# Layout transfers behind a block's first loads, gaps between scatters and expert blocks, routing spread over a block's groups, zero experts added by ScalarE

## The chip, the cores and the metric

The program runs on 1 core of one Trainium2 chip. The metric is device time in microseconds (us), median of the runs. ScalarE is called ACT here, VectorE DVE, GpSimd POOL, TensorE PE, and SP is the engine that issues plain and transposing DMAs.

## The reference, cut to what matters

A macaron layer over 32 x 256 tokens of width 128: half a mixture of experts, attention, half a mixture of experts, each on a layernormed input. Of the 12 experts 8 are real and 4 are "zero" experts, which return their input.

```python
def _L0_ffn_ref(x, gate_w, expert_bias, w1, w2):
    logits = jnp.einsum('btd,ed->bte', x, gate_w) + expert_bias
    topk_logits, topk_idx = jax.lax.top_k(logits, TOP_K)            # TOP_K = 2
    topk_w = jax.nn.softmax(topk_logits, axis=-1)
    onehot = jax.nn.one_hot(topk_idx, E_TOT, dtype=x.dtype)         # 12
    w = jnp.einsum('btk,btke->bte', topk_w, onehot)
    w_ffn = w[..., :E_FFN]                                          # 8
    w_zero = jnp.sum(w[..., E_FFN:], axis=-1)
    h = jax.nn.silu(jnp.einsum('btd,efd->btef', x, w1))
    y = jnp.einsum('btef,edf->bted', h, w2)
    out = jnp.einsum('bte,bted->btd', w_ffn, y) + w_zero[..., None] * x
    return out

x = x + 0.5 * _L0_ffn_ref(_layernorm(x), ...)
x = x + _L0_attn_ref(_layernorm(x), ...)      # 16 heads of 8, softmax over 256 keys, a fixed prior added
x = x + 0.5 * _L0_ffn_ref(_layernorm(x), ...)
```

## The kernel before

The 8192 tokens lie in SBUF as 64 tiles of 128 (`x_all`). A mixture of experts runs over **segments** of 8 or 16 tiles (`SEG`): segments 0 to 4 are the first mixture, 5 to 9 the second. Attention runs over 32 batches of 2 tiles, in a software pipeline: **turn** b holds the scores, softmax and weighted sums of batch b, the projections of batch b + 2 and the output of batch b - 1; a turn has 8 steps of 2 score tiles (`st_done` counts the tiles).

For each segment q four things happen.

- **Routing** (`route`, or in pieces inside an earlier expert block): layernorm statistics (`token_stats`, `token_moments` on DVE, `token_root` on POOL), normalised tokens and their bf16 halves `xs` (`token_norm` on DVE), gate logits (`turn_tokens`, `gate_logits` on PE, `token_cols` on ACT), top two of twelve (`first_choice`, `second_choice`), weights, counts (`count_ranks` on PE), slots (`expert_bases`, `token_slots`). Then `add_zero_experts` adds the zero experts' share to `x_all`: one DVE instruction per tile.
- **Scatter**: POOL issues 2 indirect DMAs per tile, which write `xs` rows into the DRAM buffer `xg`, sorted by expert. `spread` paces them by attention's steps, `beside_block` by a block's groups.
- **Expert block** (`experts`): 23 groups of 256 slots (15 for segments of 8 tiles). SP loads a group transposed (`load_cols`, 6 buffers), PE multiplies (`up`, L446 to L448), ACT computes silu twice (`h_f` L743, `h_hi` L745), DVE the low half (`h_lo` L1168), PE multiplies (`down`, L461 to L464), ACT evicts `y_rows` (L751), SP stores them (`store_y`, 9 groups behind the loads in SP's queue). In group g the block for q also carries a piece of the routing of the next segment.
- **Gather**: POOL fetches 2 rows per token, and DVE adds them (`combine`), at the turns that `ADDS` names.

`PHASES = {4: (2, 3), 7: (3, 4), ...}` says before which turn a block runs: block 2 (with the routing of segment 3 in it) before turn 4, block 3 before turn 7, and so on. Blocks 0, 1 come ahead of attention, 8, 9 behind it.

For each batch SP also rewrites the queries and keys through DRAM into another layout: `keep_rows` (2 stores) and `operand_rows` (6 DMAs, `k_op` and `q_in`, L353). At a block, SP's queue holds: `keep_rows`, the block's first 6 loads, the 6 layout DMAs of `operand_rows`, then the other loads and the stores:

```python
                keep_rows(b + 2)
                if b + 1 in PHASES:
                    for g in range(RX):
                        load_cols(PHASES[b + 1][0], g)
                operand_rows(b + 2)
```

Every engine works its own instructions in order, so a wait holds all that is queued behind it.

## Time and profile before

| | us |
|---|---|
| median of 3 runs | 1392.34 (1388.91 to 1397.88) |
| the profiled execution, its time | 1403.38 |
| its span | 1401.3 |
| PE busy | 1003.8 (72%) |
| DVE busy | 933.3 (67%) |
| ACT busy | 665.9 (48%) |
| POOL busy | 620.3 (44%) |
| mean granted TensorE clock | 0.88 |

The profiled execution is one run and is 11 us over the median; all stretches below are cut from it. Busy times say how full an engine is, not who sets the end: no engine is full, and each stage has to be read for the wait that ends last.

### The profile page before, as it was taken

The numbers are of one execution on the slowest core, as the hardware profiler recorded it, in microseconds if no ns is written. First come the engines' busy times: TensorE is split into PE (matmuls) and PEld (weight loads), VectorE is DVE, ScalarE is ACT, GpSimd is POOL, SyncE is SP. The second block draws the span as 40 slices with busy tenths as digits, with TensorE's granted clock in tenths as the row PEclk, the third lists the DMA queues.
The fourth block names the chain that finished last, engine by engine and source line by source line (L and its number), as shares of the span: only waits on it lengthen the run. The fifth ranks groups of instructions, "written<-read, shape, count | busy, mean of one in ns | idle before, by whom it ended". The sixth has DMA issues, their size and how long they took to land.

```text
span 1401.3 us, 37446 instructions
## 1 busy us (share of the span) xinstructions
PE 1003.8 (72%) x13558; PEld 658.8 (47%) x13558; DVE 933.3 (67%) x2505; ACT 665.9 (48%) x1356; POOL 620.3 (44%) x685
## 2 busy tenths in 40 slices
PE   1468177768776788688888888888888787775650
PEld 1346134447444744474445644444754464333540
DVE  5637476557665778578887778878688745646432
ACT  0146034346444655565555655555664554442540
POOL 2745135530555445444542555454224445541346
PEclk9979569889897989889999999999799978875985
DMA  8235812134113611262113721123431264140563
GB/s 246 70 103 126 256 41 60 54 80 107 54 52 90 139 47 58 75 143 69 47 58 72 148 73 47 58 58 81 106 84 49 84 140 101 50 86 18 117 155 74
DMA packets 248880, 125.29 MB, mean 89 GB/s; under 512 B 124384, under 2 KB 238925, under 8 KB 248448
## 3 DMA queue, kind: packets, MB, share of 16 engines
q1 hardware_dynamic: 232320, 94.01, 26.3%
q0 software_dynamic: 16384, 28.89, 8.6%
q8 instruction: 116, 1.90, 0.6%
q14 instruction: 60, 0.49, 0.1%
HBM read 36.25 MB, written 65.31 MB: 72 GB/s over the span
## 4 chain that ended last, share of the span: by engine, by line
PE 39%; DVE 25%; issue 14%; ACT 5%; POOL 5%; DMA 4%; another core or an unknown queue 4%; SPq 4%; POOLq 0%; DVEq 0%; ACTq 0%
DVE row_max L1276 9%; PE banks L573 8%; PE banks L602 4%; PE banks L548 3%; PE banks L446 3%; PE banks L448 2%; PE banks L405 2%; POOL big L888 2%; PE banks L540 2%; PE banks L447 2%; DVE h_lo L1168 2%; DMA x_cols<-xg 2%; PE banks L461 2%; PE banks L464 2%
## 5 line engine op out<-in xcount | busy, mean ns | idle before, releaser
L807 ACT ACTIVATE probs<-banks 128x512 f32<-128x512 f32 x512 | 279.5, 595 | 329.8 <-PE banks L573 301.8
L888 POOL DMA_INDIRECT big<-yg,slots x256 | 255.4, 998 | 384.2 <-ACT y_rows L751 184.9
L1276 DVE TENSOR_REDUCE row_max<-banks 128x2 f32<-128x512 f32 x512 | 330.4, 685 | 99.3 <-PE banks L573 73.2
L874 POOL DMA_INDIRECT xg<-xs,slots x256 | 259.5, 1014 | 277.5 <-PE banks L573 180.6
L1168 DVE TENSOR_TENSOR h_lo<-h_f,h_hi 128x512 bf16<-128x512 f32 x198 | 135.6, 688 | 182.1 <-ACT h_hi L745 154.5
L602 PE MATMUL banks<-probs,v_op 128*32 128x256 f32 x2048 | 196.9, 405 | 6.5 <-ACT probs L807 2.0
L461 PE MATMUL banks<-w_all,h_hi 128*128 x792 | 161.4, 231 | 52.5 <-DVE h_lo L1168 21.1
L540 PE MATMUL banks<-k_op,q_in 32*128 32x256 bf16 x1024 | 154.2, 290 | 57.8 <-DVE row_max L1276 39.9
L548 PE MATMUL banks<-q_op,k_op 32*128 32x256 bf16 x1024 | 151.3, 288 | 59.5 <-issue 45.2
L573 PE MATMUL banks<-band_parts,thirds 96*32 96x296 bf16 (+2 forms) x4096 | 184.0, 288 | 0.4 <-issue 0.4
L743 ACT ACTIVATE h_f<-banks 128x512 f32<-128x512 f32 x198 | 119.4, 603 | 130.4 <-PE banks L448 94.9
L446 PE MATMUL banks<-x_cols,w_all 128*128 128x256 bf16 x396 | 119.7, 302 | 78.0 <-DMA x_cols<-xg 47.1
L463 PE MATMUL banks<-w_all,h_hi 128*128 x792 | 157.0, 231 | 0.2
L464 PE MATMUL banks<-w_all,h_lo 128*128 x792 | 156.1, 230 | 1.3 <-issue 1.2
L573 PEld LDWEIGHTS banks<-band_parts,thirds 96*32 96x32 bf16 x4096 | 100.1, 98 | 62.1 <-issue 61.9
L751 ACT ACTIVATE y_rows<-banks 128x256 f32<-128x256 f32 x198 | 77.7, 393 | 102.6 <-PE banks L464 54.6
L448 PE MATMUL banks<-x_cols,w_all 128*128 128x256 bf16 x396 | 119.9, 303 | 0.9 <-issue 0.9
L447 PE MATMUL banks<-x_cols,w_all 128*128 128x256 bf16 x396 | 120.1, 303 | 0.4 <-issue 0.4
L745 ACT ACTIVATE h_hi<-banks 128x512 bf16<-128x512 f32 x198 | 119.4, 603 | 0.0
L461 PEld LDWEIGHTS banks<-w_all,h_hi 128*128 128x128 bf16 x792 | 82.3, 104 | 75.4 <-issue 71.3
L548 PEld LDWEIGHTS banks<-q_op,k_op 32*128 32x128 bf16 x1024 | 51.4, 92 | 130.9 <-issue 107.8
L602 PEld LDWEIGHTS banks<-probs,v_op 128*32 128x32 f32 x2048 | 81.7, 115 | 20.3 <-issue 13.3
(170 smaller groups left out, 1632.2 us busy)
## 6 DMA issues: line engine op xcount, KB each, us to landing
yg<-y_rows SPq DMA_DIRECT2D x198, 128.0 KB
k_op<-kq_kept SPq DMA_DIRECT2D x96, 64.0 KB
q_in<-kq_kept SPq DMA_DIRECT2D x96, 64.0 KB
xg<-zeros SPq DMA_DIRECT2D x2, 2944.0 KB, 14.4
xg<-xs,slots POOLq DMA_INDIRECT x256
big<-yg,slots POOLq DMA_INDIRECT x256
kq_kept<-kq_hi SPq DMA_DIRECT2D x32, 128.0 KB
kq_kept<-kq_lo SPq DMA_DIRECT2D x32, 128.0 KB
```

Source lines behind the costliest of these rows:

```text
L446: pe.matmul(o, w_hi, hi, start=True, stop=False)
L461: pe.matmul(o, h_hi[:, n % 4, cols], w_hi, start=c == 0 and j == 0, stop=False, skip_group_check=True)
L464: mm = pe.matmul(o, h_lo[:, n % 4, cols], w_hi, start=False, stop=c == 1, skip_group_check=True)
L540: return pe.matmul(banks[:, MX[v % 2], bass.ts(k, L)], q_in[r:r + 32, par, g, bass.ts(qt, P)], k_op[r:r + 32, par, g, :], start=k == 0, st ...
L548: return pe.matmul(banks[:, ST[(16 * b + u) % 3], bass.ts(k, L)], k_op[r:r + 32, par, g, bass.ts(kt, P)], q_op[r:r + 32, g, :], start=k == ...
L573: return pe.matmul(banks[32 * r:32 * r + 32, bank, :].rearrange("p (k c) -> p k c", k=2)[:, :, c0:c1], thirds[:], bc(band_parts[:, first:f ...
L602: mm = pe.matmul(banks[32 * j:32 * j + 32, PV, bass.ts(k, L)], v_op[:, par, kt, J * (2 * gp + k) + j, :], probs[:, w // 2 % 2, j, bass.ts( ...
L807: act.activation(probs[:, q % 2, u % 4, :], banks[:, ST[(16 * b + u) % 3], :], ACT.Exp).then_inc(A["exp_done"], 1)
L874: pool.indirect_dma_start(xg[q], bass.IndirectOffsetOnAxis(slots[:, q % 4, c, t:t + 1], 0), xs[:, q % 2, t, :], None, bounds_check=groups[ ...
L888: pool.indirect_dma_start(y_back[:, i, c, :], None, yg[q], bass.IndirectOffsetOnAxis(slots[:, q % 4, c, t:t + 1], 0)).then_inc(gathered[i] ...
L1168: dve.tensor_tensor(h_lo[:, n % 4, :], h_f[:, n % 3, :], h_hi[:, n % 4, :], ALU.subtract).then_inc(C["lo_ready"], 1)
L1276: dve.tensor_reduce(row_max[:, gp, :, qt, j], banks[:, MX[v % 2], :].rearrange("p (k c) -> p k c", k=2), AX.X, ALU.max).then_inc(A["max_do ...
```

## The change

1. **SP's queue.** Where a block comes next, `operand_rows` no longer stands behind the first 6 loads. It is issued inside the block, behind the load of group 12 and ahead of the store of group 3.
2. **Places.** Blocks 4 and 5 move one turn later (before turns 12 and 18), with their scatters, gathers and `ADDS`. The scatters of segments 2, 3 and 7 are spread so that they end 3 to 4 steps ahead of their block instead of at it; those of segment 4 get a whole turn.
3. **Routing inside a block.** Statistics at groups 0, 1, 3, 4 with moments per half at 2 and 5; roots per half; `token_norm` 2 tiles a group at groups 5 to 12, and the bf16 halves (`token_parts`) every second group; PE's transposes and gate logits every second group (8 to 15). First choice moves from group 13 to 16, second from 14 to 17, weights and bases to 20 (were 16 and 17), slots to 21 (were 18).
4. **Zero experts on ACT.** DVE computes a scale and a bias per token (3 small instructions a segment) and ACT adds the share: `x * scale + bias`, one ACTIVATE of 128x128 per tile. For segments 0 and 1 inside block 0 (2 a group from group 4), for 9 inside block 8, for the others in the 8 steps of the turn behind the block in which they were routed (2 a step, 1 for segment 8).

```diff
-    PHASES = {4: (2, 3), 7: (3, 4), 11: (4, 5), 17: (5, 6), 25: (6, 7), 29: (7, 8)}
+    PHASES = {4: (2, 3), 7: (3, 4), 12: (4, 5), 18: (5, 6), 25: (6, 7), 29: (7, 8)}
-    for first, q in ((11, 3), (17, 4), (23, 5)):
+    for first, q in ((12, 3), (18, 4), (24, 5)):
...
-            def experts(q, begun=0):
+            def experts(q, begun=0, b=None):
                 for g in range(groups[q] + AHEAD):
                     if begun <= g < groups[q]:
                         load_cols(q, g)
+                    if b is not None and g == AHEAD + 3:
+                        operand_rows(b)
                     if g >= AHEAD:
                         store_y(q, g - AHEAD)
...
-                    experts(PHASES[b][0], RX)
+                    experts(PHASES[b][0], RX, b + 1)
                 keep_rows(b + 2)
                 if b + 1 in PHASES:
                     for g in range(RX):
                         load_cols(PHASES[b + 1][0], g)
-                operand_rows(b + 2)
+                else:
+                    operand_rows(b + 2)
...
+            def add_zero_expert(q, t):
+                wait(act, R["zero_ready"], q + 1)
+                xt = tile_cols(SEG[q][0] + t)
+                act.activation(xt, xt, ACT.Identity, bias=z_bias[:, q % 2, t:t + 1],
+                               scale=z_scale[:, q % 2, t:t + 1]).then_inc(R["zero_added"], 1)
...
+                    if 4 <= g:
+                        for i in zero[2 * (g - 4):2 * (g - 4) + 2]:
+                            add_zero_expert(*i)
...
+                    if zero:
+                        for c in range(SEG[zero][1] // 8):
+                            add_zero_expert(zero, s * (SEG[zero][1] // 8) + c)
...
-            spread(gather_rows, 1, 0, 8, 0, 16)
-            spread(scatter_rows, 2, 0, 16, 2, 16)
-            token_root(3)
+            spread(gather_rows, 1, 0, 8, 0, 11)
+            spread(scatter_rows, 2, 0, 16, 1, 18, 3)
+            norm_turns(3, 4)
+            token_roots(3)
...
-            spread(scatter_rows, 3, 0, 16, 4, 20, 4)
+            spread(scatter_rows, 3, 0, 16, 4, 17, 4)
...
-            spread(scatter_rows, 7, 0, 16, 25, 32)
+            spread(scatter_rows, 7, 0, 16, 25, 28)
...
-            def add_zero_experts(q, k):
-                for t in range(4 * k, 4 * k + 4):
-                    xt = tile_cols(SEG[q][0] + t)
-                    i = dve.scalar_tensor_tensor(xt, xn[:, t, :], w_zero[:, t:t + 1], xt, ALU.mult, ALU.add)
-                i.then_inc(R["zero_added"], 1)
...
+                    if g in (0, 1, 3, 4) and g - (g > 2) < nk:
+                        token_stats(nxt, g - (g > 2))
+                    if g in (2, 5) and g // 5 < nk // 2:
+                        token_moments(nxt, g // 5)
+                    if 5 <= g < 5 + 2 * nk:
+                        token_norm(nxt, (g - 5) // 2, (g - 5) % 2)
+                    if 7 <= g < f - 1 and g % 2 == 1:
+                        token_parts(nxt, (g - 7) // 2)
```

SP's queue at the start of block 2, before: behind the 6 first loads stand the 6 layout DMAs, then the loads of groups 6 to 9 and the first store.

```order
L313 DMA_TRANSPOSE x_cols<-xg_0 128x2x256 x6
L353 DMA k_op<-kq_kept 32x4x256 x3
L353 DMA q_in<-kq_kept 32x4x256 x3
L313 DMA_TRANSPOSE x_cols<-xg_0 128x2x256 x4
L322 DMA yg_0<-y_rows 128x2x128
```

The same place now.

```order
L317 DMA_TRANSPOSE x_cols<-xg_0 128x2x256 x10
L326 DMA yg_0<-y_rows 128x2x128
L317 DMA_TRANSPOSE x_cols<-xg_0 128x2x256
L326 DMA yg_0<-y_rows 128x2x128
L317 DMA_TRANSPOSE x_cols<-xg_0 128x2x256
L326 DMA yg_0<-y_rows 128x2x128
L317 DMA_TRANSPOSE x_cols<-xg_0 128x2x256
L359 DMA k_op<-kq_kept 32x4x256 x3
L359 DMA q_in<-kq_kept 32x4x256 x3
L326 DMA yg_0<-y_rows 128x2x128
```

The layout DMAs moved behind 7 more loads and 3 stores.

DVE in block 2, groups 4 to 7, before: all 16 moments at once, two groups with only `h_lo`, then one quarter of the normalisation (4 tiles and both bf16 halves) behind each `h_lo`.

```order
L1168 TENSOR_TENSOR h_lo<-h_f,h_hi 128x512
L1044 BN_AGGR meanvar<-stats 128x2 x16
L1168 TENSOR_TENSOR h_lo<-h_f,h_hi 128x512 x2
L1052 TENSOR_SCALAR xn<-x_all,meanvar,rstd 128x128 x4
L1059 CAST xs<-xn 128x4x128
L1061 TENSOR_TENSOR xs<-xn,xs 128x4x128
L1168 TENSOR_TENSOR h_lo<-h_f,h_hi 128x512
```

The same engine now, from group 5 on.

```order
L1199 TENSOR_TENSOR h_lo<-h_f,h_hi 128x512
L1072 BN_AGGR meanvar<-stats 128x2 x8
L1079 TENSOR_SCALAR xn<-x_all,meanvar,rstd 128x128 x2
L1199 TENSOR_TENSOR h_lo<-h_f,h_hi 128x512
L1079 TENSOR_SCALAR xn<-x_all,meanvar,rstd 128x128 x2
L1199 TENSOR_TENSOR h_lo<-h_f,h_hi 128x512
L1079 TENSOR_SCALAR xn<-x_all,meanvar,rstd 128x128 x2
L1090 CAST xs<-xn 128x4x128
L1092 TENSOR_TENSOR xs<-xn,xs 128x4x128
L1199 TENSOR_TENSOR h_lo<-h_f,h_hi 128x512
```

The same work, in halves: one or two pieces between two `h_lo` instead of a whole quarter.

The end of block 2 on DVE, before: from the slots on, 4 zero-expert instructions behind each of the last four `h_lo`; then turn 4 begins with `row_max`.

```order
L1130 TENSOR_SCALAR slots<-slot 128x16
L1168 TENSOR_TENSOR h_lo<-h_f,h_hi 128x512
L1136 SCALAR_TENSOR_TENSOR x_all<-xn,w_zero,x_all 128x128 x4
L1168 TENSOR_TENSOR h_lo<-h_f,h_hi 128x512
L1136 SCALAR_TENSOR_TENSOR x_all<-xn,w_zero,x_all 128x128 x4
L1168 TENSOR_TENSOR h_lo<-h_f,h_hi 128x512
L1136 SCALAR_TENSOR_TENSOR x_all<-xn,w_zero,x_all 128x128 x4
L1168 TENSOR_TENSOR h_lo<-h_f,h_hi 128x512
L1136 SCALAR_TENSOR_TENSOR x_all<-xn,w_zero,x_all 128x128 x4
L1276 TENSOR_REDUCE row_max<-banks 128x2 x4
```

The end now.

```order
L1162 TENSOR_TENSOR pick<-slot_e,hot 128x192
L1163 TENSOR_REDUCE slot<-pick 128x16
L1164 TENSOR_REDUCE slot<-pick 128x16
L1165 TENSOR_SCALAR slots<-slot 128x16
L1166 TENSOR_SCALAR slots<-slot 128x16
L1199 TENSOR_TENSOR h_lo<-h_f,h_hi 128x512
L1307 TENSOR_REDUCE row_max<-banks 128x2 x4
```

The 16 zero-expert instructions are gone, and the slots stand directly ahead of the last `h_lo`.

## Rows read from the trace of the kernel before

**Rows 1.** The page: busy us and share of each engine; shares of the chain

```profile
PE 1003.8 (72%) x13558; PEld 658.8 (47%) x13558; DVE 933.3 (67%) x2505; ACT 665.9 (48%) x1356; POOL 620.3 (44%) x685
PE 39%; DVE 25%; issue 14%; ACT 5%; POOL 5%; DMA 4%; another core or an unknown queue 4%; SPq 4%; POOLq 0%; DVEq 0%; ACTq 0%
```

**Rows 2.** Windows of blocks 1 to 7: length, busy us per engine, granted clock, DMA

```profile
103.11:140.26 37.15, 30.50 (x318) 25.52 (x318) 27.17 (x86) 22.31 (x48) 18.71 (x17) 0.91 0.56 125
293.59:350.98 57.39, 46.21 (x479) 39.48 (x479) 40.60 (x131) 33.82 (x73) 3.49 (x2) 0.86 0.45 109
433.90:490.45 56.55, 45.84 (x479) 39.41 (x479) 40.86 (x132) 33.49 (x73) 26.67 (x24) 0.86 0.59 134
579.40:637.19 57.79, 45.67 (x479) 38.95 (x479) 40.58 (x131) 33.45 (x73) 25.63 (x24) 0.88 0.60 131
761.33:813.18 51.85, 40.99 (x479) 34.20 (x479) 40.59 (x131) 32.77 (x73) 26.95 (x24) 1.00 0.65 137
979.11:1034.14 55.03, 46.78 (x479) 40.43 (x479) 40.35 (x131) 34.27 (x73) 12.22 (x10) 0.85 0.47 111
1120.04:1180.73 60.69, 45.66 (x447) 37.70 (x447) 31.08 (x95) 32.40 (x71) 30.46 (x31) 0.84 0.59 131
```

**Rows 3.** PE timeline: first matmul of blocks 2, 3, 4, 5, 7, idle time before it and releaser

```profile
293.59 0.39 PE L446 MATMUL banks<-x_cols,w_all 128*128 128x256 bf16 x1 [8.26 <-DMA x_cols<-xg]
433.90 0.39 PE L446 MATMUL banks<-x_cols,w_all 128*128 128x256 bf16 x1 [7.37 <-DMA x_cols<-xg]
579.40 0.39 PE L446 MATMUL banks<-x_cols,w_all 128*128 128x256 bf16 x1 [5.41 <-DMA x_cols<-xg]
761.33 0.28 PE L446 MATMUL banks<-x_cols,w_all 128*128 128x256 bf16 x1 [1.82 <-issue]
1120.04 0.39 PE L446 MATMUL banks<-x_cols,w_all 128*128 128x256 bf16 x1 [5.29 <-DMA x_cols<-xg]
```

**Rows 4.** SP's queue around the start of block 2, then of block 5

```profile
290.93 7.78 SPq L313 DMA_TRANSPOSE x_cols<-xg  x6
298.82 2.65 SPq L353 DMA_DIRECT2D k_op<-kq_kept  x3
308.69 0.58 SPq L322 DMA_DIRECT2D yg<-y_rows  x1
...
761.45 1.89 SPq L353 DMA_DIRECT2D k_op<-kq_kept  x3
```

**Rows 5.** DVE: first choice in block 1; in block 5 first normalisation, last groups

```profile
135.52 0.35 DVE L1068 TENSOR_TENSOR logits<-banks,ebias_b 128x192 f32<-128x192 f32 x1
...
776.40 1.30 DVE L1052 TENSOR_SCALAR xn<-x_all,meanvar,rstd 128x128 f32<-128x128 f32 x4 [1.87 <-POOL rstd L856]
...
807.09 1.13 DVE L1136 SCALAR_TENSOR_TENSOR x_all<-xn,w_zero,x_all 128x128 f32<-128x128 f32 x4
808.75 1.13 DVE L1136 SCALAR_TENSOR_TENSOR x_all<-xn,w_zero,x_all 128x128 f32<-128x128 f32 x4
```

**Rows 6.** The chain that ended last, ahead of block 0

```profile
55.45 2.10 DVE x_all L1136 x8
```

**Rows 7.** SP's queue between block 1 and attention

```profile
156.87 9.94 SPq L288 DMA_DIRECT2D yg<-zeros  x1
```

**Rows 8.** Groups of instructions by form: busy, mean ns, idle before and releasers

```profile
L745 ACT ACTIVATE h_hi<-banks 128x512 bf16<-128x512 f32 x198 | 119.4, 603 | 0.0
L751 ACT ACTIVATE y_rows<-banks 128x256 f32<-128x256 f32 x198 | 77.7, 393 | 102.6 <-PE banks L464 54.6 <-remote 24.4 <-DMA yg<-y_rows 21.7
L786 ACT ACTIVATE kq_hi<-banks,bias_col 128x256 bf16<-128x256 f32 x64 | 26.9, 476 | 32.5 <-PE banks L533 21.7 <-remote 7.9 <-issue 2.7
```

**Rows 9.** Windows of turns 2, 13 and 29, columns as in Rows 2

```profile
232.30:261.80 29.50, 20.33 (x307) 10.20 (x299) 16.64 (x39) 11.31 (x23) 17.93 (x20) 1.00 0.21 63
681.00:701.50 20.50, 17.65 (x299) 9.60 (x297) 17.56 (x44) 10.95 (x22) 10.06 (x12) 1.00 0.17 52
1184.20:1214.10 29.90, 23.58 (x295) 11.71 (x295) 18.30 (x45) 11.16 (x22) 16.39 (x17) 0.79 0.15 48
```

141 lines of the change are left out of this document (76 added, 65 removed).

## The prediction

> **What bounds the kernel now.** The page comes first: PE 72%, DVE 67%, ACT 48%, POOL 44%, and a chain that is 39% PE, 25% DVE and 14% issue [rows 1]. No engine is full, so each stage has to be read by itself. Cutting the trace at the first `up` and the last `down` of a block gives 52 to 61 us for each of the six 23-group blocks [rows 2]. In them PE works 41 to 47 us, DVE 40.6 (31.1 in block 7, which routes only 8 tiles), ACT 33: engines that wait for one another. Three things stand out.
>
> First, the starts. Blocks 2, 3, 4 and 7 begin with 8.26, 7.37, 5.41 and 5.29 us of PE waiting for its first transposed load, while block 5, whose scatters had ended a turn earlier, begins after 1.82 us [rows 3]. The same blocks are also the long ones: 57.4, 56.6, 57.8, 60.7 against 51.9 and 55.0 for 5 and 6 [rows 2]. SP issues a load in 1.3 us (7.78 for six), a store in 0.58, and the six layout DMAs in about 3.9 [rows 4]; at block 2 these stand from 298.8 on between the sixth and the seventh load, just when PE has used up its six.
>
> Second, DVE inside a block: the first normalisation waits 1.87 us for POOL's root, and the zero experts take 1.05 us behind each of the last `h_lo` (1.66 us from one four to the next, 0.6 of it `h_lo`) [rows 5].
>
> Third, the turns. An ordinary one lasts 20.5 us with 10.95 of ACT and 17.6 of DVE; turn 2, with 16 scatters in it instead of 8, lasts 29.5 [rows 9].
>
> **The sum, against the profiled execution (1403.4 us, 11 over the median).**
>
> *Gaps.* The scatters end 3 to 8 steps ahead of their block, 2.6 us a step (20.5 over 8 [rows 9]), so 8 us at least, while a first load needs 2.7 from issue to landing (from 290.93 [rows 4] to 293.59 [rows 3]). So the four starts should look like block 5's: 26.3 - 4 x 1.82 = 19.0. I take **-18**, since the last scatter at block 2 was itself late. Next in line at such a start are ACT's table load and the hand-over of the banks, which the 1.82 us already hold. Bounds -12 and -19.
>
> *Late loads inside the block.* With six loads landed, blocks 2, 3, 4 and 7 should take what 5 and 6 take, 53.4 on average: 232.4 - 4 x 53.4 = **-18.7**. Part of this is TensorE's clock: granted 0.84 to 0.88 there, 1.00 in block 5 [rows 2], and in the rows of [rows 3] the first matmul takes 0.39 us after a long gap, 0.28 in block 5 (1.2 against 2.4 GHz). Block 6 shows that an early load alone doesn't secure the clock (0.85), hence the mean of both. Bounds -10 and -25.
>
> *Zero experts off DVE.* Of four portions of 1.05 us three lie ahead of the last `h_lo`, which the end of the block waits for: 3.15, less about 0.45 for the three new small instructions: -2.7 for blocks 2 to 6, -1.6 for block 7 (two portions): **-15**. The slots now stand ahead of the last `h_lo`, but that is the same work. Bound -5, if PE and SP fill the time.
>
> *Routing in halves.* The root of a half takes about half as long and starts two groups earlier, so the wait of 1.87 us goes, and no group has more than 2.5 us of DVE work until the choices. What is lost: DVE had four free groups before the choices and now has two. **-1.5** a block, **-9** for six; bounds 0 and -18.
>
> *Layout DMAs.* In the four late blocks their leaving the front is counted above; in 5 and 6 it may give 1 each. In the middle they hold up the store of group 3, for which ACT's `y_rows` of group 7 waits (4 buffers), and loads from 13 on. The loads have six buffers, some 12 us, and are covered. The store is not quite: SP needs 1.3 + 0.58 = 1.9 us per group [rows 4], a group lasts 2.0 to 2.3, so 3.9 us are made up slowly. I take +1 a block: net **+4**, bounds 0 and +23 (6 x 3.9).
>
> *Block 1.* First choice (6 instructions, 0.39 apart, the first at 135.52 [rows 5]) stood ahead of its last `h_lo` and no longer does: -2.3, and -1.2 for the root. The routing's tail behind the block gets longer, but SP needs until 166.8 to clear the buffers (the last clear is issued at 156.87 and holds its queue for 9.94 us [rows 7]), and attention waits for SP. **-3.5**, since the clears start when the block's last store has gone.
>
> *Blocks 0 and 8.* The 8 zero-expert instructions ahead of block 0, 2.10 us, are on the chain [rows 6]; at block 8 eight equal ones stand ahead of its first `h_lo`. -4.2. In exchange ACT adds inside these blocks. Cost of one: 256 elements take 393 ns plain and 476 with a bias operand, 512 take 603 [rows 8], so 128 elements with bias come to about 0.37, of which some 0.1 overlaps the next: 0.27. 24 of them are 6.5 us, half on the path: +3.3. Net **-0.9**, bounds -4 and +4.
>
> *ACT in the turns.* 16 adds are 4.3 us in turns 4, 7, 12, 18 and 25, 2.2 in turn 29: 24 us in all, in turns where ACT is idle 9.5 of 20.5 us [rows 9]. They stand behind the two exps of a step and ahead of the copies of the projections, for which DVE waits. A quarter on the path: **+6**, bounds 0 and +24. (Turn -1 has no exps and costs nothing.)
> The Trainium skill ("ScalarE: Activation LUTs", Rules for kernel authors) says that add and multiply belong on VectorE, and budgets about 0.3 us per ACTIVATE with a pointer bias plus 0.83 ns per element. That is 0.41 us here as an estimate, 36 instead of 24 us, and this term would be +9; for the 256 elements of L786 it gives 0.51 where the trace has 0.476, so it is a little high. Its advice would be a loss where ACT is the fuller engine; in the blocks it is the emptier one.
>
> *Denser scatters.* 8 more DMAs made turn 2 longer by 9 us [rows 9], 1.1 each above 8 a turn. Gathers 1 and scatters 2 and 3 were above that before and are now, with the same total (88 DMAs, begun earlier). Only segment 7's 32 go from 8 to 9.1 a turn: up to +4. I take **+1**, bounds -5 and +6.
>
> Sum: -18 - 18.7 - 15 - 9 + 4 - 3.5 - 0.9 + 6 + 1 = -54. The profiled execution would come to 1349, the median to 1392.3 - 54 = **1338**.
>
> **Rivals.**
>
> *SP's queue becomes the pace of the block* (0.17). With DVE relieved, 1.9 us per group and 3.9 in the middle hold stores back, ACT waits for `y_rows` buffers, and neither the zero experts' nor the halves' gain arrives. Then -18 - 18.7 - 3.5 - 0.9 + 6 + 1 = -34: **1358**. For it: in block 2 the first store is issued at 308.69, 15 us behind the first `up` [rows 3, 4]. Against: 17 loads, 23 stores and the layouts are 22 + 13 + 4 = 39 us, a block 50.
>
> *The waits on one another dissolve* (0.10). DVE's work in a block falls to 40.6 - 4.2 + 0.45 = 37; with 2 us ahead of its first `h_lo` and 1.3 behind its last a block could take 41. If they come to 45 on average the six save 339.3 - 270 = 69 in place of 38.7: **1308**.
>
> *The gap is not there* (0.07). POOL can't keep up in turns 1 to 6, the scatters still end at the block, and ordinary turns get longer: -54 + 18 + 10 (half of the late loads) = **1366**.
>
> *Slower: ACT's adds pull down the turns and with them the clock* (0.05). PE waits for exps in every step; turn 29 shows such a stretch, 29.9 us at 0.79 against 20.5 at 1.00 [rows 9]. Six turns at +9.4, and the adds wholly on the path (+18): -54 + 56 + 18 = +20: **1412**. It decides where the adds (0.54 us a step) exceed ACT's spare time in a step, 9.5 / 8 = 1.2 us. By rows they don't.
>
> *It doesn't do what it says* (0.02): another order, no shorter wait anywhere, 1392.
>
> **How the numbers follow.** The forecast has 0.59; its own range is 1322 to 1352. Taking in the SP rival and most of the two on either side, 8 in 10 lie between 1314 and 1368. Faster by over 1% (about what a measurement of this kernel tells from no change, 14 us): 0.88, all but the last two and a tail of the gap rival; within 1%: 0.07; slower by over 1%: 0.05.
>
> **What would show it.** Gaps: PE's idle time ahead of the first `up` about 2 us in blocks 2, 3, 4, 7, with SP's six loads behind the last scatter and ahead of the turn's end. Late loads: steps between the first ups near 1.3 to 1.6 us, a clock near 1. Zero experts: the last four `h_lo` no longer 1.66 apart. Layouts: an ACT wait for the landing of a `y_rows` store at groups 7 to 9 of over 2 us would speak for the SP rival. Turns: turn 12 and 18 over 22 us would speak for the ACT rival. Blocks at 48 to 51 us confirm the sum; at 53 or more it is wrong in the terms on DVE.

## The result: 1401.7 us, and the profile after

The changed kernel took 1401.71 us (median of 17 executions, 1391.98 to 1410.65), the kernel before 1392.34 beside it (17, 1385.02 to 1401.64): ratio 1.0077, 95% interval 1.0054 to 1.0101. I had forecast 1338, in a range of 1314 to 1368. The profiled execution of the change has a span of 1393.2 us and so is one of its shortest; single executions of either kernel scatter by some 10 us, so below spans show where time lies, and ratios say how much.

One thing has to be known to read the numbers. The experiments ran in five sets, each beside the kernel before. In three sets that kernel took 1387 to 1394 us, in two 1293 and 1298, and one chip met both. I call these the 1390 level and the 1295 level, and compare ratios only within one. (The expectations, written while this came out, speak of a slower and a faster chip; the times in them are for the 1390 level unless they say otherwise.) The change itself was measured at the 1390 level alone.

The page of the change, against [rows 1]:

```profile
PE 1015.3 (73%) x13558; PEld 665.0 (48%) x13558; DVE 903.1 (65%) x2407; ACT 711.3 (51%) x1484; POOL 623.3 (45%) x697
PE 42%; DVE 21%; issue 14%; ACT 8%; another core or an unknown queue 4%; SPq 4%; DMA 4%; POOL 3%; DVEq 0%; POOLq 0%; ACTq 0%
```

DVE has lost 30 us of work and a sixth of its part in the chain, ACT has gained 45. The windows of blocks 2 to 7, columns as in [rows 2]:

```profile
292.00:348.10 56.10, 45.12 (x479) 39.76 (x479) 36.26 (x118) 33.35 (x74) 4.67 (x4) 0.86 0.42 102
432.30:488.00 55.70, 43.08 (x479) 37.48 (x479) 38.04 (x124) 33.10 (x73) 28.93 (x27) 0.92 0.61 135
590.90:648.80 57.90, 46.02 (x479) 39.84 (x479) 36.77 (x118) 33.32 (x73) 28.18 (x27) 0.85 0.59 122
772.30:829.80 57.50, 46.59 (x479) 39.61 (x479) 36.56 (x118) 33.27 (x73) 28.78 (x27) 0.85 0.56 124
974.40:1028.90 54.50, 44.41 (x479) 38.53 (x479) 36.74 (x118) 33.47 (x74) 20.39 (x20) 0.88 0.55 122
1118.90:1174.20 55.30, 41.86 (x447) 34.80 (x447) 28.97 (x90) 32.60 (x71) 31.25 (x31) 0.91 0.73 151
```

337.0 us against 339.3: DVE works 3.7 us less in a full block, and the blocks together are as long as before. The granted clock rose in blocks 3, 6 and 7 and fell in 4 and 5, and block 5, the model of my forecast, went from 51.9 to 57.5. The gaps ahead of them did go. PE's first matmuls of blocks 2 and 5, against [rows 3]:

```profile
292.04 0.28 PE L453 MATMUL banks<-x_cols,w_all 128*128 128x256 bf16 x1 [1.82 <-issue]
...
772.33 0.39 PE L453 MATMUL banks<-x_cols,w_all 128*128 128x256 bf16 x1 [1.82 <-issue]
```

Inside a block two places are new. The first is at groups 11 and 12 (timeline of block 5 around the layout transfers, SP, ACT and DVE only):

```profile
786.05 1.89 SPq L359 DMA_DIRECT2D k_op<-kq_kept  x3
...
787.98 1.90 SPq L359 DMA_DIRECT2D q_in<-kq_kept  x3
...
789.92 0.59 SPq L326 DMA_DIRECT2D yg<-y_rows  x1
...
792.24 0.38 ACT L765 ACTIVATE y_rows<-banks 128x256 f32<-128x256 f32 x1 [3.07 <-DMA yg<-y_rows]
...
795.82 0.60 ACT L757 ACTIVATE h_f<-banks 128x512 f32<-128x512 f32 x1 [3.20 <-remote]
...
796.94 0.69 DVE L1199 TENSOR_TENSOR h_lo<-h_f,h_hi 128x512 bf16<-128x512 f32 x1 [5.47 <-ACT h_hi L759]
```

The six transfers hold SP's queue from 786.05 to 789.88, the next store of `y` leaves at 789.92, and ACT's next `y_rows` has waited 3.07 us for its landing. Behind it ACT waits 3.20 us more for something that the trace doesn't name, and DVE's next `h_lo` comes after 5.47 us of nothing. The step from one `up` to the next is 6.7 to 8.6 us long there in blocks 2 to 5, where the kernel before had 2.6 to 2.9.

The second is the end of a block (DVE's timeline, block 3):

```profile
479.29 0.69 DVE L1199 TENSOR_TENSOR h_lo<-h_f,h_hi 128x512 bf16<-128x512 f32 x1 [1.68 <-ACT h_hi L759]
479.89 0.17 DVE L1124 TENSOR_SCALAR wts<-tanh_gap 128x16 f32<-128x16 f32 x1
...
482.57 0.15 DVE L1151 TENSOR_TENSOR base<-ends,scan 128x8 f32<-128x8 f32 x1
482.75 0.69 DVE L1199 TENSOR_TENSOR h_lo<-h_f,h_hi 128x512 bf16<-128x512 f32 x1
483.36 0.32 DVE L1154 TENSOR_REDUCE owner_f<-past 1x23 f32<-1x184 f32 x1
...
485.65 0.74 DVE L1199 TENSOR_TENSOR h_lo<-h_f,h_hi 128x512 bf16<-128x512 f32 x1
```

and PE's, beside it:

```profile
483.59 0.23 PE L468 MATMUL banks<-w_all,h_hi 128*128 x1 [2.14 <-DVE h_lo L1199]
...
486.53 0.29 PE L468 MATMUL banks<-w_all,h_hi 128*128 x1 [2.03 <-DVE h_lo L1199]
```

PE has done its last `up` at 480.8. Weights and bases (2.8 us) stand between the last but two and the last but one `h_lo`, slots (2.3 us) between that and the last, and PE waits for both. From the last `up` to the end of a block it is 7.1 us on average over blocks 2 to 7, 5.3 before.

Last the turns, columns as in [rows 9]: turns 2, 5 and 13.

```profile
238.20:268.00 29.80, 21.35 (x297) 11.20 (x297) 17.76 (x40) 11.16 (x22) 16.82 (x19) 0.87 0.18 57
379.40:405.10 25.70, 20.30 (x292) 11.21 (x295) 14.94 (x34) 11.10 (x23) 13.69 (x16) 0.80 0.15 46
...
671.70:692.60 20.90, 18.06 (x307) 9.65 (x297) 17.94 (x44) 10.94 (x23) 10.13 (x12) 1.00 0.20 56
```

Turn 13 has 8 of GpSimd's indirect DMAs in it, turn 5 has 12, turn 2 has 15. The seven stretches from the end of a block to the start of the next took 807.0 us before and 804.0 after. Four shorter gaps are -18.8 in that, so the turns took back some 16 (14 by the profiles of the same two kernels in e9 and e10 below).

### The profile page after: what moved, and what is told of

It reads as the page before. It is cut to its first block, busy times and chain, and to the rows that moved or that the text cites. A ratio compares the mean times of both kernels' runs of the same rounds, so it can differ in the third digit from the quotient of the medians.

```text
span 1393.2 us, 37528 instructions
## 1 busy us (share of the span) xinstructions
PE 1015.3 (73%) x13558; PEld 665.0 (48%) x13558; DVE 903.1 (65%) x2407; ACT 711.3 (51%) x1484; POOL 623.3 (45%) x697
## 4 chain that ended last, share of the span: by engine, by line
PE 42%; DVE 21%; issue 14%; ACT 8%; another core or an unknown queue 4%; SPq 4%; DMA 4%; POOL 3%; DVEq 0%; POOLq 0%; ACTq 0%
PE banks L581 9%; DVE row_max L1307 8%; PE banks L610 5%; PE banks L556 3%; PE banks L453 3%; PE banks L455 3%; PE banks L412 2%; PE banks L454 2%; ACT probs L825 2%; PE banks L548 2%; PE banks L468 2%; PE banks L471 2%; PE banks L470 2%; POOL big L913 2%
## 5 line engine op out<-in xcount | busy, mean ns | idle before, releaser
L913 POOL DMA_INDIRECT big<-yg,slots x256 | 258.2, 1009 | 343.0 <-ACT y_rows L765 157.7
L899 POOL DMA_INDIRECT xg<-xs,slots x256 | 256.2, 1001 | 283.9 <-PE banks L581 177.7
L610 PE MATMUL banks<-probs,v_op 128*32 128x256 f32 x2048 | 203.1, 413 | 14.6 <-ACT ot_sb L818 5.9
L581 PE MATMUL banks<-band_parts,thirds 96*32 96x296 bf16 (+2 forms) x4096 | 189.5, 294 | 1.4 <-issue 1.4
L581 PEld LDWEIGHTS banks<-band_parts,thirds 96*32 96x32 bf16 x4096 | 103.4, 100 | 66.2 <-issue 66.0
```

What stands on the lines that cost most here:

```text
L581: return pe.matmul(banks[32 * r:32 * r + 32, bank, :].rearrange("p (k c) -> p k c", k=2)[:, :, c0:c1], thirds[:], bc(band_parts[:, first:f ...
L610: mm = pe.matmul(banks[32 * j:32 * j + 32, PV, bass.ts(k, L)], v_op[:, par, kt, J * (2 * gp + k) + j, :], probs[:, w // 2 % 2, j, bass.ts( ...
L899: pool.indirect_dma_start(xg[q], bass.IndirectOffsetOnAxis(slots[:, q % 4, c, t:t + 1], 0), xs[:, q % 2, t, :], None, bounds_check=groups[ ...
L913: pool.indirect_dma_start(y_back[:, i, c, :], None, yg[q], bass.IndirectOffsetOnAxis(slots[:, q % 4, c, t:t + 1], 0)).then_inc(gathered[i] ...
```

## The experiments

Every kernel is the kernel before with some of the four parts of the change: **gaps** (GpSimd's order, starts of blocks 4 and 5), **layout** (the six transfers with group 12), **halves** (routing in pieces), **zero** (ACT's zero experts). Ratios are to the kernel before in the same set; "blocks" is the sum of blocks 2 to 7, "tail" the mean from last `up` to block end in them, "stretches" the seven stretches from block to block, all from the profiled execution.

| run | kernel | us | ratio, 95% | blocks | tail | stretches |
|---|---|---|---|---|---|---|
| **1390 level** | before | 1392.3 | 1 | 339.3 | 5.3 | 807.0 |
| | the change | 1401.7 | 1.0077 (1.0054 to 1.0101) | 336.9 | 7.1 | 804.0 |
| e1 | less layout | 1395.5 | 1.0021 (0.9992 to 1.0050) | 330.1 | 7.8 | 802.5 |
| e2 | less gaps | 1410.7 | 1.0122 (1.0086 to 1.0158) | 343.7 | 7.4 | 813.2 |
| e3 | less halves | 1380.9 | 0.9909 (0.9878 to 0.9939) | 311.6 | 4.5 | 815.9 |
| e4 | less zero | 1394.2 | 1.0026 (0.9995 to 1.0057) | 332.3 | 6.6 | 804.5 |
| e9 | the change | 1390.3 | 1.0007 (0.9976 to 1.0039) | 339.9 | 7.5 | 799.6 |
| e10 | before | 1379.1 | 0.9946 (0.9916 to 0.9977) | 334.1 | 5.4 | 801.5 |
| e11 | gaps, zero | 1369.9 | 0.9864 (0.9827 to 0.9901) | 313.5 | 4.3 | 809.1 |
| e12 | e11, late steps | 1384.3 | 0.9985 (0.9954 to 1.0015) | 331.1 | 7.6 | 797.8 |
| e17 | the change, dense | 1423.8 | 1.0255 (1.0215 to 1.0295) | 341.6 | 7.4 | 838.0 |
| e18 | gaps, zero from 2, layout last | 1364.5 | 0.9851 (0.9816 to 0.9885) | 305.9 | 4.6 | 801.3 |
| **1295 level** | | | | | | |
| e5 | halves | 1313.8 | 1.0121 (1.0087 to 1.0156) | 327.6 | 7.0 | 747.8 |
| e6 | gaps, layout | 1265.8 | 0.9760 (0.9729 to 0.9791) | 312.4 | 5.0 | 714.7 |
| e7 | gaps, zero | 1256.5 | 0.9667 (0.9625 to 0.9708) | 303.2 | 3.8 | 715.5 |
| e8 | gaps | 1261.9 | 0.9725 (0.9681 to 0.9768) | 307.0 | 5.0 | 716.0 |
| e13 | e7, dense | 1255.4 | 0.9708 (0.9663 to 0.9754) | 301.1 | 3.8 | 710.2 |
| e14 | gaps, zero from 2 | 1251.7 | 0.9685 (0.9640 to 0.9730) | 300.8 | 3.8 | 710.0 |
| e15 | e14, layout last | 1243.1 | 0.9618 (0.9567 to 0.9669) | 301.0 | 4.5 | 717.9 |
| e16 | e14, scatters paced | 1255.3 | 0.9708 (0.9665 to 0.9750) | 306.4 | 3.7 | 716.9 |

e10 is the kernel before, instruction for instruction, and came out at 0.9946; e9 is the change once more and came out 0.7% below its first ratio. So a difference under some 0.7% between two kernels, interval or not, isn't told apart here.

**e1, layout transfers back at the front.**

```diff
-                    experts(PHASES[b][0], RX, b + 1)
+                    experts(PHASES[b][0], RX)
...
-                else:
-                    operand_rows(b + 2)
+                operand_rows(b + 2)
```

> The change, with one part undone: the six layout transfers go out behind a block's first six loads again, and not with group 12. Theory 1 (the transfers in the middle hold back the y stores, ACT's y_rows and PE's down, 6.7 to 8.6 us at groups 11 to 12 of each 23-group block, against the 4 to 5 us that the late loads took at group 6): the step at groups 11 to 12 falls to 3 us, a stall of 4 to 5 us comes back at group 6, the blocks 2 to 7 are 2 to 4 us shorter each: 1402 - 12 to 24 = 1378 to 1390. Rival (the stall in the middle is PE's and ACT's own, from the routing work there, and the layouts only stand beside it): it stays, the late loads come back on top, 1402 + 6 x 3 = 1420.

Measured 1.0021, 1395.5 us, between the theory's 1378 to 1390 and the rival's 1420. The step of 6.7 to 8.6 us at groups 11 to 12 is gone (2.6 and 2.5 in blocks 2 and 3), steps of 3.4 and 3.9 at group 5 and of 5.8 and 4.5 at group 9 stand there instead, and the blocks are 7 to 10 us shorter in sum. Theory 1's direction in the blocks, and less than its size (12 to 24); the ratio, against 1.0077 and 1.0007 of the change, doesn't settle it.

**e2, the gaps back.** GpSimd's program, `PHASES`, `ADDS` and `store_out(5)` as before:

```diff
-    PHASES = {4: (2, 3), 7: (3, 4), 12: (4, 5), 18: (5, 6), 25: (6, 7), 29: (7, 8)}
+    PHASES = {4: (2, 3), 7: (3, 4), 11: (4, 5), 17: (5, 6), 25: (6, 7), 29: (7, 8)}
```

> The change, with one part undone: scatters, norms, gathers and the starts of blocks 4 and 5 stand where they stood before. Theory 2 (the gap ahead of a block is gone for good, and it was worth some 3 us a block): the gaps come back, 1402 + 18 = 1420. Rival (what the gaps gave was given back in the turns, whose scatters are denser now): within 5 us of 1402. Rival 2 (the denser turns cost more than the gaps): under 1395.

Measured 1.0122: the closed gaps are worth 6 to 16 us here, of a term of 18. The four waits are back at 6.2, 5.9, 5.3 and 5.2 us. The late seventh load is not (the step at group 5 is 1.3 to 1.5 us in blocks 2 to 5, 1.8 to 5.5 before): the layout transfers no longer stand ahead of it, so this run says nothing on the late loads' 18.7.

**e3, routing whole again.** `token_moments`, `token_root`, `token_norm` and the group numbers as before:

```diff
-                    if nk and g == f:
+                    if nk and g == 13:
                         first_choice(nxt)
-                    if nk and g == f + 1:
+                    if nk and g == 14:
                         second_choice(nxt)
```

> The change, with one part undone: the routing of the next tokens beside a block is done in whole steps again (moments once at group 4, norms of four tiles, turns and gate at groups 8 to 12, choices at 13 and 14, count at 17, weights, bases and slots at 16, 17, 18). Theory 3 (choices and count stand two groups apart instead of three and PE waits for the chosen experts near group 19, some 5.5 to 6 us a step instead of 4): 4 blocks x 2 us and the stall in the middle lighter, since the turns of the tokens are over by then: 1390 to 1396. Rival (as predicted before the run, the halves take 9 us away): 1411.

Measured 0.9909, 14 to 23 us faster than the change, far over what any theory gave; the blocks are 25 us shorter. Its DVE at the end of block 3:

```profile
471.96 0.69 DVE L1281 TENSOR_TENSOR h_lo<-h_f,h_hi 128x512 bf16<-128x512 f32 x1
472.57 0.33 DVE L1222 TENSOR_REDUCE owner_f<-past 1x23 f32<-1x184 f32 x1
...
474.78 0.17 DVE L1234 TENSOR_SCALAR slots<-slot 128x16 int32<-128x16 f32 x1
474.86 1.89 DVE L1281 TENSOR_TENSOR h_lo<-h_f,h_hi 128x512 bf16<-128x512 f32 x3
```

The slots end with four groups still to come, and three `h_lo` follow back to back: PE and ACT had run ahead, and DVE catches up. With no group ahead of it there is nothing to catch up, and PE waits for each instruction.

**e4, zero experts on DVE.**

```diff
-            experts(0, None, [(q, t) for q in range(2) for t in range(8)])
+            experts(0)
...
+                if z <= g < z + nk:
+                    add_zero_experts(nxt, g - z)
```

> The change, with one part undone: DVE adds the zero experts again, behind the slots of a block (in blocks 2 to 7 from group 22 on). Theory 4 (ACT's adds cost 5 us in block 0 and 2 to 3 us in each of the turns behind a block, and DVE had room for them): 1402 - 15 = 1387. Rival (as predicted, DVE's adds at the block's end hold the last groups, 15 us less 6 us of turns): 1411.

Measured 1.0026. Block 0 is 38.0 us long (42.1 and 42.4 in the change, 37.4 before). The stretches are 804.5, as with ACT's adds (804.0 and 799.6): in the turns they cost nothing that can be seen. The ratio can't be told from the change's.

**e5, halves alone.** Before, with `token_moments`, `token_root`, `token_norm` and the group numbers of the change.

> The kernel before with one part of the change: routing in halves (and its later choices, count, weights and slots); gaps, layout transfers and zero experts as before. Theory 3, as e3_no_pieces sharpened it (the halves themselves cost 23 us, by the steps at groups 19 to 20, 5.3 to 6.0 against 4.1, and by the last group's way from its up to the block's end, 7.7 to 8.5 against 3.7): slower by 15 to 23 us, 1407 to 1417; with DVE's zero experts moved behind the slots the tail of a block may grow to 9. Rival (the cost arises only where the halves meet the layout transfers in the middle, steps of 6.7 to 8.6 at groups 11 to 12): within 5 us of before. Prediction's own step: 9 us faster.

Measured 1.0121: theory 3, without any layout transfer in the middle. The tail is 7.0 us. In this set the gap of the kernel before could be seen too, at block 2:

```profile
267.70 0.39 PE L458 MATMUL banks<-x_cols,w_all 128*128 128x256 bf16 x1 [14.11 <-DMA x_cols<-xg]
```

It is 14.11 us, not 8.26 as in [rows 3]: turn 3's exps are done in 16.9 us there and took 23.7 in the kernel before, and the scatters ordered beside them are the same.

**e6, gaps and layout.** As e3, with DVE's zero experts.

> The kernel before with two parts of the change, gaps and layout transfers; routing whole, DVE adds the zero experts. Beside e3_no_pieces (1381) it lacks only ACT's adds. Theory 4 (ACT's adds cost 4.7 us in block 0 and 2 to 3 us in each turn behind a block): 1374. Rival (with the routing whole, DVE's adds stand at groups 19 to 22 and cost the block's end 1.4 us or more each, as its 5.1 us from the last up to the end against 3.7 says): 1385 to 1388.

**e7, gaps and zero.** As e3, with the layout transfers at the front.

> The kernel before with two parts of the change, gaps and ACT's zero experts; routing whole, layout transfers behind the first six loads. Beside e3_no_pieces (1381) the layout transfers are back. Theory 1 (in the middle they hold back y stores, worth 8 us as e1_no_layout measured it): 1373. Rival (their cost in the middle arose with the halves only, and with the routing whole the late loads at group 6 cost more than they): 1390 or over.

**e8, gaps alone.**

> The kernel before with one part of the change: the gaps (scatters, norms, gathers, starts of blocks 4 and 5). Theory 2 (three us a block, five blocks, less some in the turns): 1394 - 6 to 18 = 1376 to 1388. Rival (given back in the turns): within 5 us of 1394.

Measured 0.9760, 0.9667, 0.9725. Gaps alone are worth 2.7%, 36 us. That is not twice their term of 18: with the gap goes a part of the late loads as well, and the two terms are 36.7 together. The waits themselves are 11.3 us in e8 and 32.3 in e5, so 21 us shorter, although block 3 still waits 5.8 us; what the rest is can't be read off, since the kernel before has no profile at this level. ACT's zero experts on top are worth 0.6%, the layout transfers in the middle cost 0.35%; both are under the 0.7% that can be told apart. The first matmul of block 2 in e8:

```profile
254.10 0.28 PE L458 MATMUL banks<-x_cols,w_all 128*128 128x256 bf16 x1 [1.83 <-issue]
```

**e9 and e10, the change and the kernel before again.** Word for word.

> The changed kernel, word for word, once more, beside the other three kernels on one chip. On one chip the kernel before took 1394 us and on another 1298, and parts that were timed on only one of them can't be set against the whole. If the chip's own pace decides what the change is worth (rival: the price of dense scatters beside the turns is that of the slower chip alone), then on a chip where the kernel before takes 1298 us the change is 1 to 2% faster (gaps and zero experts together gave -3.3%, the halves alone +1.2%); where it takes 1394 us the ratio is 1.008 again. If the parts add up the same way everywhere, it is 1.008 on either.

> The kernel before, word for word, for its profile on this chip; its time is that of before, ratio 1.00. If this chip takes 1298 us, the turns 2 to 6, which took 26 to 29 us each in the profile of before, are some 20 us here, and the waits that the trace could name nobody for are gone; if it takes 1394, they are as they were.

This set was at the 1390 level again: 1.0007 and 0.9946, 0.6% between the two, near the 0.8% of the first measurement. What e9 expected of the change at the 1295 level stays untested.

**e11, e7 again, and e12, late steps.**

> The kernel e7_gaps_zero once more (gaps, and the zero experts on ACT; routing whole, layout transfers behind the first six loads). On the chip of before at 1298 us it gave 0.967; on the chip of 1394 us e3_no_pieces, with the layout transfers moved as well, gave 0.991. If the gain of the gaps is given back only on the slower chip: 0.985 to 0.990 there, 0.967 on the faster one.

```diff
-                        if nk and g == 13:
+                        if nk and g == 12 + nk:
                             first_choice(nxt)
-                        if nk and g == 14:
+                        if nk and g == 13 + nk:
                             second_choice(nxt)
-                        if nk and g == 16:
+                        if nk and g == 16 + nk:
                             weights(nxt)
-                        if nk and g == 17:
                             expert_bases(nxt)
-                        if nk and g == 18:
+                        if nk and g == 17 + nk:
                             token_slots(nxt)
```

> e11 with one edit: the choices at groups 16 and 17, the count at 19, weights and bases together at 20, slots at 21, as in the change, but norms, turns and moments whole, as before. Theory 3a (what the halves cost is the lateness of the last steps: DVE's weights and bases, 2.8 us, and slots, 2.4 us, stand between the last two h_lo of a block, behind PE's last ups): slower than e11 by 15 us or more, steps of 5.3 to 6.0 at groups 19 to 20 and 7.7 us from last up to block end. Theory 3b (it is the turns of tokens spread over groups 8 to 15, two groups apart): within 5 us of e11.

e11 gave 0.9864, within the 0.985 to 0.990 expected, and e12 0.9985: +1.2%, 17 us, from the place of five steps alone (PE's count and ACT's `weigh` moved with them). Blocks in sum, e12 and then e11:

```profile
sum 331.10, PE 256.41 PEld 219.78 DVE 215.44 ACT 198.30 POOL 135.27; mean PE 42.74 PEld 36.63 DVE 35.91 ACT 33.05 POOL 22.55
```

```profile
sum 313.60, PE 254.32 PEld 216.24 DVE 213.88 ACT 197.96 POOL 132.77; mean PE 42.39 PEld 36.04 DVE 35.65 ACT 32.99 POOL 22.13
```

The same work on every engine within 4 us (DVE's within 1.6), and 17.5 us more of length. Theory 3a.

e7 and e11 are one kernel at the two levels. Block 0, turn 5 and turn 13 of e11:

```profile
58.69:102.28 43.59, 29.42 (x270) 20.89 (x270) 11.40 (x18) 25.43 (x60) 21.80 (x26) 0.80 0.42 95
373.20:397.80 24.60, 20.09 (x293) 11.49 (x295) 15.53 (x35) 11.33 (x23) 13.40 (x16) 0.80 0.13 40
664.70:685.30 20.60, 17.93 (x306) 9.71 (x298) 17.99 (x43) 10.94 (x22) 10.15 (x12) 1.00 0.19 56
```

and of e7:

```profile
58.65:87.75 29.10, 26.14 (x270) 19.95 (x270) 11.41 (x18) 25.28 (x60) 21.30 (x25) 1.00 0.59 143
337.90:356.30 18.40, 17.14 (x304) 9.49 (x298) 15.41 (x35) 11.08 (x23) 14.13 (x15) 1.00 0.25 76
602.00:622.00 20.00, 17.41 (x306) 9.64 (x298) 17.38 (x43) 11.05 (x22) 10.13 (x12) 1.00 0.18 55
```

The turn with 8 indirect DMAs is nearly equal at both (20.6, 20.0). Turn 5, with 12 of them in e11 and 14 in e7, and block 0, beside which 16 scatters stand back to back, are 6 and 14 us longer at the 1390 level. In e11's block 0 PE, ACT and SP stand still while GpSimd issues:

```profile
70.56 0.58 SPq L331 DMA_DIRECT2D yg<-y_rows  x1
...
73.69 0.37 PE L460 MATMUL banks<-x_cols,w_all 128*128 128x256 bf16 x1 [0.32 <-issue]
79.36 0.38 ACT L776 ACTIVATE y_rows<-banks 128x256 f32<-128x256 f32 x1 [8.94 <-remote]
80.03 0.29 PE L473 MATMUL banks<-w_all,h_hi 128*128 x1 [5.97 <-issue]
...
80.84 1.20 SPq L322 DMA_TRANSPOSE x_cols<-xg  x1
```

```profile
74.88 0.98 POOL L924 DMA_INDIRECT xg<-xs,slots  x1 [0.30 <-issue]
...
77.45 0.98 POOL L924 DMA_INDIRECT xg<-xs,slots  x1 [0.30 <-issue]
```

The DMA at 77.45 is GpSimd's last there. ACT, idle for 8.94 us, goes on 0.9 us behind its end, PE 0.7 us behind ACT, and SP, which had issued nothing since 71.14, at 80.84: it is not PE alone that waits.

Counting the indirect DMAs between the first exp of a turn and the first of the next, and averaging the turns' lengths (us):

| in a turn | 8 | 12 | 13 | 14 | 15 | 16 | 17 |
|---|---|---|---|---|---|---|---|
| 1390 level (before, change, e10, e11) | 20.5 | 23.4 | 26.0 | 25.2 | 28.3 | 29.5 | 30.8 |
| 1295 level (e7, e8) | 19.7 | 20.3 | 19.8 | 20.3 | | | 21.1 |

Turns that end in a block (3, 6 and so on) are not in it.

**e13 and e17, the same scatters in half the turns.** In e7, and then in the change:

```diff
-            spread(scatter_rows, 5, 0, 16, 13, 32)
+            spread(scatter_rows, 5, 0, 16, 13, 16)
+            norm_turns(15, 17)
...
-            spread(scatter_rows, 6, 0, 16, 19, 32)
+            spread(scatter_rows, 6, 0, 16, 19, 16)
+            norm_turns(21, 23)
```

> e11_gaps_zero_again with one suspected cost doubled: the 32 scatters of blocks 5 and 6 are spread over two turns each (16 a turn) and not over four (8 a turn); their number stays. Theory 5 (a turn grows by some 1.1 us for each indirect DMA above 8 on a chip where before takes 1390 us): four turns get 8 more and grow from 20.5 to 29 us, four get none and shrink from 20.4 to 18.5: + 26 us, 1.005 of before if e11 is 0.986. On a chip where before takes 1298 us: within 6 us of e7. Rival (the dense turns are long for other work in them, ACT's adds or the start behind a block): within 6 us of e11 on any chip.

> The changed kernel with the one edit of e13_dense: the 32 scatters of blocks 5 and 6 spread over two turns each, 16 a turn. Where before takes 1390 us (theory 5, 1.1 us for each indirect DMA above 8 in a turn, less 2 us for each turn that has none): + 26 us on the 1.001 to 1.008 of the change, 1.020 to 1.027; rival (the dense turns are long for other work in them): 1.001 to 1.008. Where before takes 1293 us the edit costs nothing (e13_dense against e14_zero_from_2: 4 us, within their intervals), and the time is the change's own: gaps -2.7%, zero experts -0.6%, halves +1.2%, layouts in the middle +0.3%, sum 0.98; if the parts don't add, 1.00 or over.

e13 met the 1295 level: 0.9708 against 0.9667 and 0.9685, no cost that can be told; its four dense turns take 19.8 to 19.9 us. e17 met the 1390 level: 1.0255 against 1.0077 and 1.0007, 25 to 34 us, within the 1.020 to 1.027 expected. Its turns 13 to 16:

```profile
673.60:702.80 29.20, 21.84 (x307) 11.14 (x299) 17.85 (x43) 11.28 (x23) 17.98 (x20) 0.87 0.20 63
702.80:731.80 29.00, 21.62 (x297) 11.53 (x297) 18.93 (x44) 11.15 (x23) 17.81 (x20) 0.83 0.16 50
731.80:752.40 20.60, 17.66 (x291) 10.19 (x294) 17.06 (x42) 11.16 (x23) 2.13 (x4) 0.92 0.07 21
752.40:770.90 18.50, 17.16 (x303) 9.43 (x298) 15.54 (x35) 11.05 (x23) 2.08 (x4) 1.00 0.12 38
```

The four dense turns (13, 14, 19, 20, with 15 to 17 DMAs) take 29.2, 29.0, 27.2 and 33.1 us, and took 20.9, 20.4, 20.8 and 20.4 in the change with 8. The four turns left with none (15, 16, 21, 22) take 20.6, 18.5, 22.0 and 18.5, and took 20.4, 20.0, 21.3 and 19.3. So the price of density is shown by an edit: 9.0 us a turn for the second eight, 0.3 for the first, at the one level and not at the other.

**e14, zero experts on ACT only from block 2 on.**

```diff
-            experts(0, None, [(q, t) for q in range(2) for t in range(8)])
+            experts(0)
```

and `route` of DVE adds those of 0 and 1 ahead of block 0.

> e11 with one edit: DVE adds the zero experts of blocks 0 and 1 in the opening, as before; ACT does those of 2 to 9. Block 0's later steps of 2.0 us fall to 1.3 (8 steps, 5 us), and the opening takes 2 us more: 3 us faster than e11. Rival (block 0 is held by the scatters anyway): no change.

**e15 and e18, layout transfers behind the last load.**

```diff
-                    if b is not None and g == AHEAD + 3:
+                    if b is not None and g == 23:
```

> e14 with one edit: the six layout transfers go out behind a block's last load (with group 23), neither ahead of the seventh load nor with group 12. If they cost where they stand (ahead: a late seventh load, 3 to 5 us at groups 5 to 6; middle: held y stores), nothing waits for them there, and each of 6 blocks gains 2 to 4 us: 12 to 24 us faster than e14. Rival (the stalls at groups 5 to 10 are PE's issue beside other transfers, not the queue's order): within 5 us of e14.

> e15_layout_last once more. Where before takes 1390 us: e11's 0.986, less what the transfers behind the last load take away from the stalls at groups 5 to 10 (12 us) and 3 us in blocks 0 and 1: 0.975. Where before takes 1293 us: 0.962 again.

**e16, the scatters beside block 0 paced.**

```diff
-            scatter_rows(1, 0, 8)
             attention_constants()
+            beside_block(scatter_rows, 1, 0, 8, 0, "hi_ready", False)
```

> e14 with one edit: the 16 scatters of block 1, which stand back to back ahead of GpSimd's constants beside block 0, go out one to each group of block 0, as those of block 9 beside block 8. Where before takes 1390 us: block 0 falls from 43 to 35 us or less (1.3 us a scatter is the densest stretch of all, PE stood still for 6 us in it), 8 us faster than e14. Where before takes 1298 us: no change. Rival (each scatter costs the same wherever it stands): no change on either.

e14 0.9685: block 0 is 26.4 us and not 29.1, but the total can't be told from e7's. e15 0.9618, 8.6 us below e14 with intervals that overlap slightly, where 12 to 24 were expected; blocks 2 and 3 are 5.3 and 2.0 us shorter, blocks 4 and 6 longer. e18, the same kernel at the 1390 level, 0.9851 where 0.975 was expected, can't be told from e11. e16 0.9708: nothing gained at the 1295 level, where nothing was to be gained by theory 5; at the other it wasn't tried. This kernel has the lowest time at either level, 3.8% (e15) and 1.5% (e18) under the kernel before, though neither can be told from its neighbours.

## Why the prediction was wrong

**The step that failed most: "Routing in halves", -9 with bounds 0 and -18.** It cost 14 to 23 us in the change (e3), 16 alone (e5). The prediction looked at how even the halves are ("no group has more than 2.5 us of DVE work until the choices") and named what is lost as two free groups. What the halves take is the end of the schedule: turns of tokens at a pitch of two groups put the choices at 16 and 17, the count at 19, weights with bases at 20, slots at 21, of 23 groups. There PE's `up`s are done or nearly so, nobody has a lead, and each DVE instruction is on the path. e12 moves only these steps and gets +17. Where the halves give and take can be read from the starts of the groups' `up`s (us, mean of blocks 2 to 6):

| | group 0 to 8 | 8 to 13 | 13 to 16 | 16 to the end |
|---|---|---|---|---|
| before | 15.5 | 17.7 | 5.0 | 17.5 |
| the change | 12.4 | 16.5 | 6.8 | 20.6 |
| e1 (halves, layout in front) | 12.7 | 15.0 | 6.4 | 20.1 |
| e3 (routing whole, layout in the middle) | 14.6 | 14.8 | 5.0 | 16.6 |
| e11 (routing whole, layout in front) | 13.7 | 16.2 | 5.1 | 16.3 |
| e12 (e11, late steps) | 13.9 | 15.5 | 5.0 | 20.6 |

Against e3 the change gains 2.2 us a block in the first eight groups, so the evenness that the prediction counted on was worth its 1.5 a block and more. It loses 1.8 at groups 13 to 16, into which PE's turns of tokens were drawn out, and 4.0 behind group 16, where e12 has the same 20.6. The other 1.7, at groups 8 to 13, come only where halves and layout transfers meet: with the routing whole the transfers in the middle cost nothing (e3 against e11, both at the 1390 level).

**"Zero experts off DVE", -15.** It had taken DVE's 3.15 us off a tail in which they were last. In the change they left and the slots came: "the same work", the prediction said of those, and so it was, on the path where it hadn't been. With the routing whole the tail falls from 5.3 to 3.8 and 4.3 (e7, e11), 1 to 1.5 us a block, not 2.5; e7 against e8 gives 0.6%, 5 to 8 us, for the whole edit, just under what can be told apart.

**"ACT in the turns", +6, and "Blocks 0 and 8", -0.9.** In the turns no cost of the adds can be seen (stretches 804.5 in e4 against 804.0 and 799.6; 716.0 in e8 against 715.5 in e7), but the stretches of kernels whose GpSimd issues the same DMAs at the same places scatter by 8 us at the 1295 level and by 18 at the 1390 level, so the +6 isn't excluded. Block 0 paid 4 to 6 us for them, against the 2 saved ahead of it. The sum took 0.27 us an add, which was too little: two of them take 0.86 us back to back in a turn of e3, one by itself 0.50. The Trainium skill ("ScalarE: Activation LUTs", Rules for kernel authors), by whose budget the prediction had estimated 0.41, was nearer. So the price of an add was too low by a third or more, and the total doesn't show it; that ACT had room in the turns is the likely reason, and it isn't shown.

**"Gaps", -18, and "Denser scatters", +1 with bounds -5 and +6.** The mechanism of the gaps was right and the size, too: idle time ahead of blocks 2, 3, 4 and 7 fell by 18.8 us. But only a part arrived. Against the kernel before the stretches gave back 14 to 16 us; against e2, the change with its gaps back, 2 to 6. The price of density is the prediction's own (1.1 us for each DMA above 8 a turn), and its count holds nearly: "with the same total" is true of turns 0 to 6, which have 32 of them before and after, and the whole comes from 44 to 49. At 1.1 us the 5 more are 5.5 us, at the edge of its bounds. What it left out is where they stood. Before, 12 of the 44 were in turns 3 and 6, which end in a wait for the block; there GpSimd's last DMAs fell into a time in which PE had nothing to do. After, 4 are in those turns and 45 in turns without a block, which had 32. Turn 6 has 12 DMAs in both kernels and lasts 27.1 and 27.2 us, although its gap is 5.5 us shorter. So closing a gap seems to bring the price of the DMAs that it had covered; this is read from the turns, and no run isolates it. At the 1295 level the price is near nothing, and there gaps and late loads bring what the two terms say.

**"Late loads inside the block", -18.7.** In the change the late seventh load is gone (the step at group 5 is 1.3 us in blocks 2 to 4, 4.5 to 5.5 before), and the tail and the middle cover it up. With the routing whole it can be seen in the blocks: 2, 3, 4, 7 take 209.2 us in e3 against 232.4 in [rows 2], -23, of which some 9 are other edits' (blocks 5 and 6, which had no late load, are 2.2 us shorter each), and e11 against e10 gives -22. So the term held in the main.

**"Layout DMAs", +4 with bounds 0 and +23.** The wait that the prediction named is the one that came (ACT's `y_rows` for a store's landing, 3.07 us), with 3.2 us of an unnamed wait behind it. e1's blocks are 7 to 10 us shorter in sum, so the term was rather +7 to +10 beside the halves, and about nothing without them (311.6 in e3 against 313.5 in e11); in the ratio it is within what isn't told apart. Sending them behind the last load (e15, e18) gave 0 to 9 us.

**Block 1, -3.5**: 33.0 and 35.1 us in the change and e9 against 37.2 and 36.6: -1.6 to -4.1, about as forecast.

Put with what was measured (halves +14 to +23, zero experts -5 to -8, layouts +7 to +10, blocks 0 and 8 +1 to +2, block 1 -2 to -4, ACT in the turns 0 to +6, denser scatters +5 to +16, late loads -14 to -22, gaps -18) the sum lies between some -25 and +18 us, and holds the +1 to +9 of the two measurements of the change. The largest single miss, 23 to 32 us of some 60, is the halves'. The prediction's own sign of a wrong sum, blocks of 53 us or more, came: they are 56.2 on average.

**The rivals.** "SP's queue becomes the pace" had the place of one wait right and its consequence (neither the zero experts' nor the halves' gain arrives), but not the cause: with SP relieved (e1) the loss stays, with the routing whole (e3) it goes. The rival on the slower side, ACT's adds in the turns, did not happen. "The gap is not there" named longer ordinary turns, but by a POOL that can't keep up; POOL did. No rival had a longer block by the halves, and their measured price lies outside the term's bounds of 0 and -18.

**Open:** what makes PE, ACT and SP stand still at the 1390 level while GpSimd issues indirect DMAs, and what sets the level: one chip had both. PE's rows say "issue", ACT's an unknown releaser ("remote"). The trace has the program's own instruction transfers among its DMA packets, equally many and equally long at both levels, so their number is not it.

## What to carry to other kernels

A step that is moved to even out an engine's work should be costed by where the chain's last steps land, not by the largest portion left: here an instruction ahead of the middle of a block was absorbed by the lead that the other engines have, and from group 20 on it counted in full. When a wait is closed, ask what it covered: work that stood in it may have to be paid once the wait is gone. When transfers are moved and their price begins at a threshold, count those above it stretch by stretch, those of the stretches with a wait too. And four edits at once hid what two of them give alone (1.4% at the 1390 level): measure the parts.
